# Window mixing: transposing as pairs of 64-row tiles, every bias addition on ScalarE, normalisation on GpSimd in long pieces

## The reference, cut to what matters

```python
def _L0_conv_ref(x, w, b):            # WS = 8, SHIFT = 4, HEADS = 16
    x = jnp.pad(transpose(x, (0, 2, 3, 1)), 4 on every side)
    xw = windows of 8x8 pixels        # (windows, 16 heads, 64 pixels, 16 channels)
    y = jnp.einsum('nhjd,hij->nhid', xw, w) + b[None, :, :, None]
    return y without the padding, as (B, C, H, W)

x = x + _L0_conv_ref(_gn(x), L0_conv_w, L0_conv_b)     # _gn: group norm, 32 groups of 8 channels
x = x + _L1_conv_ref(_gn(x), ...)                      # attention; the change leaves it alone
```

## Time and profile before

| what | us |
|---|---|
| median of 3 runs | 2488.25 (2484.59 to 2489.66) |
| the profiled execution | 2490.49 |
| its span in the trace | 2488.8 |
| granted TensorE clock, mean | 0.984 |
| window mixing, first to last instruction | 0 to about 260 |

### The profile page before, as it was taken

The page is one execution under the profiler, slowest core; times in us unless marked ns, Lnnn a source line. Parts: engine busy times, 40 slices in busy tenths (PEclk is TensorE's granted clock), DMA queues, the critical chain, the costliest instruction groups (busy, mean ns, idle before and its releaser), DMA issues. The chain is left out here.

```text
span 2488.8 us, 66780 instructions
## 1 busy us (share of the span) xinstructions
PE 2364.8 (95%) x25485; PEld 1886.2 (76%) x25485; DVE 1992.4 (80%) x2652; ACT 1495.8 (60%) x1864; POOL 1099.0 (44%) x1477
## 2 busy tenths in 40 slices
PE   5999799999999999799999999999999889999998
PEld 5889687777787788577888888888888656666666
DVE  7887588787688786788888888888888578888775
ACT  5777576665566566566677677667767433443342
POOL 6722387787787787300000000000000068888887
PEclk9999899999999999899999999999999999999999
DMA  7874688988889889988888888888888677777774
GB/s 283 342 293 177 212 301 313 325 294 306 307 281 323 320 282 321 267 204 204 206 213 208 208 208 210 207 207 212 210 206 209 215 251 271 279 278 271 270 271 135
DMA packets 300877, 628.38 MB, mean 252 GB/s; under 512 B 50688, under 2 KB 252160, under 8 KB 291456
## 3 DMA queue, kind: packets, MB, share of 16 engines
q1 hardware_dynamic: 295616, 590.90, 77.1%
q10 hardware_dynamic: 4048, 31.11, 3.5%
q0 software_dynamic: 1008, 3.67, 0.4%
HBM read 327.81 MB, written 300.94 MB: 253 GB/s over the span
## 5 line engine op out<-in xcount | busy, mean ns | idle before, releaser
L1901 POOL TENSOR_TENSOR ql<-image,qh 128x1024 fp32r<-128x1024 f32 x128 | 305.3, 2410 | 971.4 <-ACT qh L1929 971.4
L1555 PE MATMUL c_ps<-dh,wh 128*128 128x512 f32 x1152 | 463.5, 402 | 17.5 <-DVE wl L1706 13.1
L1470 ACT ACTIVATE dh<-image 128x1632 fp32r<-128x1632 f32 x192 | 301.5, 1570 | 266.7 <-PE c_ps L1555 250.6
L1555 PE MATMUL c_ps<-dh,wl 128*128 128x512 f32 x1152 | 455.0, 395 | 0.0
L1555 PE MATMUL c_ps<-dl,wh 128*128 128x512 f32 x1152 | 453.6, 394 | 1.3 <-issue 1.3
L1664 DVE TENSOR_TENSOR dl<-image,dh 128x1632 fp32r<-128x1632 f32 x192 | 356.4, 1856 | 72.2 <-ACT dh L1470 72.2
L1125 PE MATMUL o_ps<-xh,wqh 128*128 128x512 f32 x768 | 320.8, 418 | 11.0 <-issue 7.6
L1125 PE MATMUL o_ps<-xl,wqh 128*128 128x512 f32 x768 | 304.6, 397 | 0.0
L1125 PE MATMUL o_ps<-xh,wql 128*128 128x512 f32 x768 | 303.4, 395 | 0.0
L1555 PEld LDWEIGHTS c_ps<-dh,wh 128*128 128x128 f32 x1152 | 217.7, 189 | 70.1 <-DVE wl L1706 13.2
L1555 PEld LDWEIGHTS c_ps<-dl,wh 128*128 128x128 f32 x1152 | 217.3, 189 | 53.4 <-issue 1.3
(11 more groups left out here) (210 smaller groups left out, 5024.0 us busy)
## 6 DMA issues: line engine op xcount, KB each, us to landing
qkv_scratch<-stage SPq DMA_DIRECT2D x384, 408.0 KB, 4.0
image<-qkv_scratch SPq DMA_DIRECT2D x189, 816.0 KB, 6.3
qr_scratch<-qs SPq DMA_DIRECT2D x128, 256.0 KB, 3.0
yq_scratch<-qy SPq DMA_DIRECT2D x64, 512.0 KB, 6.7
image<-qr_scratch SPq DMA_DIRECT2D x128, 256.0 KB, 6.2
image<-yq_scratch SPq DMA_DIRECT2D x128, 256.0 KB, 5.9
ox<-x_scratch SPq DMA_DIRECT2D x8, 4096.0 KB, 14.8
out<-ox SPq DMA_DIRECT2D x7, 4096.0 KB, 12.7
```

What stands on the lines that cost most here:

```text
L1470: act.activation(dh[kind][:, :], raw[kind], ACT.Copy).then_inc(hi_ready, 1)
L1555: last = pe.matmul(c_ps[:, m, :], w[hp][:, kind, part, o:o + P], cells[:, :, HALF * dy:HALF * dy + HALF * NB], start=(k == 0), stop=(k == 5))
L1901: pool.tensor_tensor(two_of(ql, n, tp), two(n, tp), two_of(qh, n, tp).bitcast(F32), ALU.subtract)\
```

## The change

Four things change, all within window mixing:

1. `turn` and `turn_back` transpose blocks of 64 partitions instead of 128. The lower and the upper 64 rows of the array are used as two tiles, one after the other in program order, and each writes a PSUM bank of its own. One 128x128 transpose becomes two of 64 rows with 64 moving columns.
2. The swap of window rows moves from the normalisation of ct = 1 into `turn_back` (`halves[v ^ ct]`), and `turn_back` writes PSUM in the order of the image's rows, in runs of eight. `add_back` adds in 512 and 448 element pieces, and twice as many of them.
3. All eight `add_bias` banks are ScalarE's (`BY_DVE` and `BY_ACT` go).
4. Normalisation is GpSimd's from the second image on, in four long pieces a step: two inner ones of 128 x 1792 and two edges of 128 x 256. ScalarE keeps two inner pieces of the first half and one of the second half of the first image.

The diff, cut to its core:

```diff
-        xT = sb("xT", [P, GP, C])
+        xT = sb("xT", [P, 2, GP * CT, HC])
...
-        BY_DVE = ((0, 0), (1, 0))
-        BY_ACT = [(k, half) for k in range(QUADS) for half in range(2) if (k, half) not in BY_DVE]
+        N_R = 2 * QUADS
...
-                src = src[:, :, SHIFT:W - SHIFT].rearrange("p r (s c) -> p s r c", c=WS)
-                dst = dst[:, 0:WINS - 1, :, :]
-                if ct == 1:
-                    src, dst = src[:, :, WS * w:WS * w + WS, :], dst[:, :, WS * (w ^ 1):WS * (w ^ 1) + WS, :]
+                src, dst = src[:, :, SHIFT:W - SHIFT].rearrange("p r (s c) -> p s r c", c=WS), dst[:, 0:WINS - 1, :, :]
             else:
-                c0, y0 = (0, W - SHIFT) if what == "right" else (SHIFT, 0)
-                src, dst = src[:, :, y0:y0 + SHIFT], dst[:, WINS - 1, :, c0:c0 + SHIFT]
-                if ct == 1:
-                    src = src.rearrange("p (t v r) c -> p t v r c", v=2, r=WS)[:, :, w, :, :]
-                    dst = dst.rearrange("p (t v r) c -> p t v r c", v=2, r=WS)[:, :, 1 - w, :, :]
+                src = src.rearrange("p r (k c) -> p k r c", c=SHIFT)[:, ::1 - W // SHIFT, :, :]
+                dst = dst[:, WINS - 1, :, :].rearrange("p r (k c) -> p k r c", c=SHIFT)
...
-        def rows_by_act(b, g):
-            return WR if (b, g) == (0, 0) else 2 if g == 0 else 1
+        PARTS = [(0, "inner"), (1, "inner"), (0, "edges"), (1, "edges")]
 
         def act_parts(b, g):
-            return [(0, "inner", 0)] + [(1, "inner", w) for w in range(rows_by_act(b, g))]
+            return PARTS[0:2 - g] if b == 0 else []
 
         def pool_parts(b, g):
-            return [(1, "inner", w) for w in range(rows_by_act(b, g), WR)] + EDGES
+            return [p for p in PARTS if p not in act_parts(b, g)]
...
-                if s + 2 < len(STEPS):
-                    normal_slots(*STEPS[s + 2])
...
-                    pe.wait_ge(m_taken, len(BY_DVE) * (s - 1) + k + 1)
-                    pe.wait_ge(m_taken_act, len(BY_ACT) * (s - 1) + k + 1)
+                    pe.wait_ge(m_taken, N_R * (s - 1) + 2 * k + 2)
                 if f >= 2:
                     pe.wait_ge(t_taken, N_T * s + f - 1)
+
                 for a in range(4):
                     column, row = 2 * f + a // 2, GR * g + 2 * WS * (a % 2)
                     for ct in range(CT):
-                        o = (a % 2) * C + ct * P
-                        last = pe.transpose(ps[:, pair(f) + a // 2, o:o + P],
-                                            xn[:, ct, column, row:row + 2 * WS, :].rearrange("p r c -> p (r c)"),
-                                            K["ident"][:, :])
+                        o = (CT * a + ct) * HC
+                        for ch in range(2):
+                            last = pe.transpose(ps[:, pair(f) + ch, o:o + HC],
+                                                xn[halves[ch], ct, column, row:row + 2 * WS, :].rearrange("p r c -> p (r c)"),
+                                                K["ident"][halves[ch], halves[ch]])
...
-                                cells = xT[halves[row], :, MIX_CH * h:MIX_CH * h + MIX_CH]\
-                                    .rearrange("p (s t) c -> p s t c", t=2)
+                                per, c0 = HC // MIX_CH, MIX_CH * (h % (HC // MIX_CH))
+                                cells = xT[halves[row], h // per % 2, :, c0:c0 + MIX_CH]\
+                                    .rearrange("p (s t k) c -> p s t k c", t=2, k=CT)[:, :, :, half, :]
                                 weights = wT[halves[row], :, (h - row) % MIX_HEADS, :]
-                                whole = 1 if g == GROUPS - 1 and row != half else 2
+                                whole = 1 if g == GROUPS - 1 and row == 1 else 2
...
-                    last = pe.transpose(ps[:, 4 + 2 * (n % 2) + a // 4, P * (a % 4):P * (a % 4) + P],
-                                        yT[:, a0 + a, P * ct:P * ct + P], K["ident"][:, :])
+                    for v in range(2):
+                        cells = ps[:, 4 + 2 * (n % 2) + v, :].rearrange("p (t r s c) -> p t r s c", t=2, r=WS, c=WS)[:, a % 2, :, a // 2, :]
+                        rows = halves[v ^ ct]
+                        last = pe.transpose(cells, yT[rows, a0 + a, P * ct:P * ct + P], K["ident"][rows, rows])
...
-                back = ps[:, bank:bank + 2, :].rearrange("p q n -> p (q n)").rearrange("p (s r c) -> p r s c", s=4, c=WS)
-                img = rows_of(b, ct)[:, GR * g:GR * g + GR, :]
-                inner = 4 - n % 2
-                c0 = SHIFT + 4 * WS * (n % 2)
-                mid = img[:, :, c0:c0 + WS * inner].rearrange("p r (s c) -> p r s c", c=WS)
-                last = dve.tensor_tensor(mid, mid, back[:, :, 0:inner, :], ALU.add)
-                if inner < 4:
-                    for c, y in ((0, W - SHIFT), (SHIFT, 0)):
-                        edge = img[:, :, y:y + SHIFT]
-                        last = dve.tensor_tensor(edge, edge, back[:, :, inner, c:c + SHIFT], ALU.add)
+                back = ps[:, bank:bank + 2, :].rearrange("p v (t r x) -> p v t r x", t=2, x=W // 2)
+                img = rows_of(b, ct)[:, GR * g:GR * g + GR, :].rearrange("p (t v r) x -> p v t r x", t=2, v=2)
+                x0 = SHIFT + W // 2 * (n % 2)
+                inner = min(W // 2, W - x0)
+                for v in range(2):
+                    mid = img[:, v, :, :, x0:x0 + inner]
+                    last = dve.tensor_tensor(mid, mid, back[:, v, :, :, 0:inner], ALU.add)
+                    if inner < W // 2:
+                        edge = img[:, v, :, :, 0:W // 2 - inner]
+                        last = dve.tensor_tensor(edge, edge, back[:, v, :, :, inner:W // 2], ALU.add)
```

More of the change, by code:

```diff
@@ L306, in window_mixing @@
         N_T, N_M, N_K = FILLS, QUADS, BACKS
+        halves = (slice(0, HC), slice(HC, P))
         STEPS = [(b, g) for b in range(B) for g in range(GROUPS)]
-        BY_DVE = ((0, 0), (1, 0))
-        BY_ACT = [(k, half) for k in range(QUADS) for half in range(2) if (k, half) not in BY_DVE]
+        N_R = 2 * QUADS
         def dram_rows(r0, r1):
@@ L364, in _, with part @@
                     load(b + 3, GR * g, GR * g + GR, x_loaded[(b + 3) % 2][g])
-        def part(op, b, g, ct, what, w):
+        def part(op, b, g, ct, what):
             src, sc, nb = rows_of(b, ct)[:, GR * g:GR * g + GR, :], T["sc"][:, ct:ct + 1], T["nb"][:, ct:ct + 1]
@@ L423, in normal_slots @@
                 at_least(pool, t_full, N_T * (GROUPS * (b - 1) + g + 1))
-                for ct, what, w in pool_parts(b, g):
-                    last = part(normal, b, g, ct, what, w)
+                for ct, what in pool_parts(b, g):
+                    last = part(normal, b, g, ct, what)
                 last.then_inc(edge_ready, 1)
@@ L451, in normal_slots @@
                 at_least(act, t_full, N_T * (GROUPS * (b - 1) + g + 1))
-                for ct, what, w in act_parts(b, g):
-                    last = part(normal, b, g, ct, what, w)
+                for ct, what in act_parts(b, g):
+                    last = part(normal, b, g, ct, what)
                 last.then_inc(xn_ready, 1)
@@ L459, in fill @@
                 act.wait_ge(t_full, N_T * s + f + 1)
-                act.activation(xT[:, 4 * f:4 * f + 4, :].rearrange("p a c -> p (a c)"),
-                               ps[:, pair(f):pair(f) + 2, :].rearrange("p a n -> p (a n)"), ACT.Copy).then_inc(t_taken, 1)
+                act.activation(xT[:, :, 8 * f:8 * f + 8, :].rearrange("p r a c -> p r (a c)"), ps[:, pair(f):pair(f) + 2, :],
+                               ACT.Copy).then_inc(t_taken, 1)
             def add_bias(s, k, half):
@@ L471, in add_bias @@
                                           ACT.Identity, bias=bias[:, h:h + 1])
-                last.then_inc(m_taken_act, 1)
+                last.then_inc(m_taken, 1)
             norm_std(act, 0, T, ns)
@@ L484, in _ @@
                 at_least(act, k_full, N_K * s)
-                for k, half in BY_ACT:
-                    add_bias(s, k, half)
+                for k in range(QUADS):
+                    for half in range(2):
+                        add_bias(s, k, half)
                 image = chain_at(b, g)
@@ L498, in _ @@
         def _(pe):
-            halves = (slice(0, WS * WS), slice(WS * WS, P))
             def links(b):
@@ L584, in _ @@
                 if means:
-                    pe.wait_ge(m_taken, len(BY_DVE) * s + 1)
+                    pe.wait_ge(m_taken, N_R * s + 1)
                     means()
@@ L674, in _ @@
             dve.wait_ge(b_ready, 1)
-            def add_bias(s, k, half):
-                dve.wait_ge(m_full, N_M * s + k + 1)
-                h = MIX_HEADS // 2 * half + 2 * k
-                out = yT[:, :, MIX_CH * h:MIX_CH * (h + 2)].rearrange("p a (h c) -> p h a c", h=2)
-                src = ps[:, 2 * k + half, :].rearrange("p (h a c) -> p h a c", h=2, c=MIX_CH)
-                bb = bias[:, h:h + 2].unsqueeze(2).unsqueeze(3).broadcast_to([P, 2, GP, MIX_CH])
```

(4 more changed lines are left out.)

13 lines of the change are left out of this document (6 added, 7 removed).

## The result

The changed kernel is slower. Its median is 2502.66 us (2494.24 to 2510.33, 7 runs) against 2489.66 us (2484.59 to 2491.81, 7 runs) of the kernel before; the ratio is 1.0055, 95% interval 1.0041 to 1.0068. Forecast were 2485.8 us and a range of 2479 to 2492. The profiled execution took 2502.73 us (span 2501.0), where the one before took 2490.49 (2488.8).

What follows compares the result with a forecast made beforehand. No engine was full; a chain passing from engine to engine bounded the first 260 us. Chain gain -8.5 and clock falls +6.0 gave -2.5: 2490.49 became 2488.0, and the median, 2.2 lower, 2485.8 us; range 2479 to 2492.

Steps and rivals of the forecast that it cites:

- The chain: Window mixing's engine-to-engine sequence between first fills, at full clock: 27.4 us an image instead of 28.45, 8.5 us in all.
- (f) to (i): Second half of an image: wait for add_back 0.93, add_backs and turn_backs 3.69, first activation 1.39, until next fill 6.0.
- (a): First half: fills 0 and 1, square root and scale, until the first add_back; 3.56 us, before 4.00.
- (b): First half: two add_backs, until TensorE may do the last turn_back; 3.24 us, before 3.13.
- (c): First half: the last turn_back, until mixing starts; 0.45 us, before 1.03.
- (d): First half: mixing of the first four heads, until ScalarE takes them; 2.15 us, as before.
- (e): First half: ScalarE's bias activations, until the next fill 0; 6.0 us, before 5.60.
- (g): Second half: add_backs and TensorE's last two turn_backs, until mixing; 3.69 us, before 4.17.
- (i): Second half: from the first bias activation until the next fill 0; 6.0 us, before 5.18.
- what the clock does: First halves of seven images: TensorE idles, its clock falls to 1.2 GHz in most; 0.85 us each, 6.0 in sum.
- The rival for "slower": Mixing's second halves: the clock falls there too, up to 15 falls; 2493 to 2499 us, chance 0.15.

Runs made afterwards that it cites:

- e8: Changed kernel with unread matmuls in each image's first half and 16 small matmuls (64 instructions) at the idle start; 2490.0 us.
- e13: Changed kernel with unread matmuls in the first halves and normalisation shared between ScalarE and GpSimd as before the change; 2490.6 us.
- e6: Changed kernel with normalisation cut and shared between ScalarE and GpSimd as before the change; 2502.4 us.
- e2: Changed kernel with two of the eight banks of each half emptied by VectorE again, six by ScalarE; 2494.0 us.
- after_again: The changed kernel run again without any edit; the total came again, and the next stage began at 268.0 us, 1.2 us earlier.
- e14: Control of e1: the same unread matmuls at the same places, each with 2 columns; the work in them is worth 4.3 us.
- e1: Changed kernel with matmuls that nobody reads added on TensorE in each image's first half, to fill its waits; 2490.2 us.
- e12: Changed kernel with loads of images 3 to 7 bringing one row of pixels per piece, all stores kept; total changed by 6 us.
- e11: Changed kernel with 32 small matmuls (128 instructions) at the start, where TensorE is idle; 2494.6 us.

## Why the prediction was wrong

**The chain was right.** Steps (f) to (i) from 147.40: 1.10, 3.91, 1.37 and 5.86, sum 12.24, forecast 0.93, 3.69, 1.39 and 6.0. For a first half without a low stretch e8 serves, from 40.90: (a) 3.57, (b) 3.25, (c) 0.64, (d) 1.94, (e) 5.87, sum 15.27; forecast 3.56, 3.24, 0.45, 2.15 and 6.0, sum 15.4. (c) and (g) are a little long because sixteen transposes take 0.50 from the start of one group to the start of the next (147 to 151 us), forecast 0.45, and the last group ends only after 0.71. `add_back` takes 1.28 and 1.4 where 1.18 and 1.30 were put. GpSimd's long pieces:

```profile
L409 POOL TENSOR_SCALAR xnorm<-image,m_sc,m_nb 128x1792 f32<-128x1792 f32 x25 | 45.7, 1835 | 79.9 <-DVE m_nb L148 79.8
...
L409 POOL TENSOR_SCALAR xnorm<-image,m_sc,m_nb 128x256 f32<-128x256 f32 x26 | 14.1, 552 | 0.0
```

1.835 and 0.552 for 1.83 and 0.56; that they are hidden, e13 bears out and e6 leaves open. So an undisturbed image would take 27.5. The full-clock gain of about 8 us is an estimate from there, and no run shows it: e8 with no low stretch has 8.9 us of standstills in a mixing of 233.7, against 232.3 before, and without them it would be 224.8.

**ScalarE's banks.** The losses in (e) and (i) are real, but that giving two banks back to VectorE would return 1.2 us an image did not come true: in e2 no undisturbed second half is shorter, and first halves are shorter by 0.6. The rule of the Trainium skill that I weighed there ("TensorEngine Tiling (Array Packing)", PSUM Bottleneck) is borne out by that run in part at most. VectorE pays for the two banks in the same chain, ahead of its additions, which I take for the reason; no run isolates it.

**The step that failed: what the clock does.** I put "a fall in most first halves", at half of 1.7 us each, 6.0 in sum. There was one in every first half (two in the first of them, two of the eight 6.8 us long; in `after_again` seven in six first halves, four of them 6.8 us long). The first halves are 16.85 in the mean against 15.67 in e8, or 15.3 without the three standstills that e8 has in them: 1.2 to 1.55 each, 8 to 11 in sum. The term had the right sign and place and was too small by 2 to 5 us. It holds in these profiles; the pair of kernels that isolates the clock (e14 against e1) gives 4.3 us for the total, so its cost there isn't settled to better than a factor of two.

**The term that was missing: the bounds of instruction blocks.** This is the larger step that failed: I counted the transposes' time and not their number, and put the fetching of instructions at nothing. It took 5.2 us in three second halves, and 6.3 us in a later stage that I had called unchanged. Of the 14.7 us between the forecast -2.5 and the measured +12.2 of the two spans these are 11.5, and what the first halves took more than 15.4 + 0.85 is another 4.2. The rival for "slower" (falls in second halves too) was not what happened: what lengthened second halves were standstills, and the one low stretch at 118.8 begins where such a one ends (118.76). That rival's 2493 to 2499 would have been too low as well.

**What stays open.** Why a packet starts late. The standstills stay without most of the images' loads (e12); that it stands behind the stores is a guess from one sight (in the changed kernel the store of 228.4 to 233.5 us ends as the packet starts), and not shown. And of single profiles: the mixing of one kernel scatters by 1.5 us (242.1, 240.7), so of differences of 1 or 2 us in the table nothing should be made.

## What to carry to other kernels

Splitting a TensorE operation in two is not free when its time halves: the instructions double, and in a burst a block of 256 is used up in 4 to 6 us, faster than a late one comes. Count instructions per microsecond beside microseconds, and look for idle time of TensorE that ends on "issue". Waits are instructions too, and a loop's jump back can cost as much as several late blocks. When an edit gains or loses more than its own stretch explains, run a control with the same instructions and no work in them, and one that only shifts the program: here up to 128 instructions at an idle place moved the total by up to 8 us, more than half of what the change under test did.

## What the hardware showed unexpectedly

TensorE's instruction blocks: 100 of 100 standstills at one place modulo 256 instructions, resumed 2.17 to 2.68 us after the packet's start. 128 instructions more in the first 20 us of the program changed the standstills near 650 us from 10.5 us to 4.7 (e11). A loop's jump back stopped TensorE for 4.0 to 5.9 us in all 20 traces, once in each, while packets of instructions started; the sixteen branches of later loops took up to 0.2. And two 64-row tiles of transposes run side by side: sixteen at a pace of 0.50 us, where eight 128-row ones needed 0.87.
